# The last shared unit's second GEMM as three rounded products instead of native fp32, and the masks built in the first shared unit

## What is computed

```python
# layer 0: a softmax map from ctx, then a mixture of 8 experts and one shared expert
x = x + softmax(layernorm_affine(sim(layernorm(x), ctx)))
xt = layernorm(x)
top_p, top_i = top_k(softmax(xt @ gate_w), 2)      # each expert takes 160 slots per choice
h = gelu(buf[e] @ w1[e] + b1[e])                   # 256 -> 1024
y = h @ w2[e] + b2[e] + gelu(buf[e] @ wd[e]) @ wu[e]
sh = gelu(xt @ sw1 + sb1) @ sw2 + sb2 + gelu(xt @ swd) @ swu
x = x + sum_k(top_p[k] * y[expert k]) + 0.2 * sh
# layer 1: attention scores from ctx times layernorm(x), masked, softmax
scores = (ctx @ Wq.T + bq) @ (ctx @ Wk.T + bk).T / 8 * layernorm(x)
x = x + softmax(where(mask_SxS2 | mask_BxS2, -inf, scores))
# then a gated FFN whose weights are looked up in a table of 16
x = x + (silu(xn @ gate.T) * (xn @ up.T)) @ down.T
```

## Time and profile before

| | |
|---|---|
| median of three runs | 328.35 us |
| the profiled execution | 328.0 us, its span 326.3 us |
| TensorE busy (matmul) | 305.4 us, 94% of the span |
| VectorE, ScalarE, GpSimd busy | 239.2, 151.3, 111.6 us |
| mean granted TensorE clock | 0.965 |
| chain that ended last, by engine | PE 78%, DVE 9%, POOL 4%, ACT 3% |

### The profile page before, as it was taken

The page is one execution under the profiler, slowest core; times in us unless marked ns, Lnnn a source line. Parts: engine busy times, 40 slices in busy tenths (PEclk is TensorE's granted clock), DMA queues, the critical chain, the costliest instruction groups (busy, mean ns, idle before and its releaser), DMA issues.

```text
span 326.3 us, 6015 instructions
## 1 busy us (share of the span) xinstructions
PE 305.4 (94%) x1944; PEld 262.5 (80%) x1944; DVE 239.2 (73%) x650; ACT 151.3 (46%) x358; POOL 111.6 (34%) x153
## 2 busy tenths in 40 slices
PE   8998567997999999999999999999999989979995
PEld 4654355776989899898989999899888879879994
DVE  3658987413499989898998989898986749866632
ACT  2466437533346455564546555565633532541210
POOL 7473644770000605032150604123062226234331
PEclk9998769999899999999999999999999999979998
DMA  7994018335167664939375574828033000010101
GB/s 230 371 265 105 7 42 268 123 113 148 48 178 249 142 220 97 308 63 294 94 212 167 129 252 72 294 52 229 3 40 131 1 0 2 0 35 0 34 1 64
DMA packets 26259, 41.48 MB, mean 127 GB/s; under 512 B 3898, under 2 KB 16955, under 8 KB 26236
## 3 DMA queue, kind: packets, MB, share of 16 engines
q1 hardware_dynamic: 22012, 36.46, 35.2%
q0 software_dynamic: 4224, 4.75, 8.2%
HBM read 31.37 MB, written 9.82 MB: 126 GB/s over the span
## 4 chain that ended last, share of the span: by engine, by line
PE 78%; DVE 9%; POOL 4%; issue 3%; ACT 3%; DMA 1%; SPq 0%; POOLq 0%
PE hb L715 25%; PE yb L734 24%; PE hb L849 10%; PE yb L748 5%; PE tb L648 3%; PE rb L864 3%; PE yb L553 2%; POOL xbuf_dram L498 2%; PE yb L864 1%; DVE x L1249 1%; DVE bst L1104 1%; DVE xn L1110 1%; DVE xT_lo L1262 1%; POOL rstd L461 1%; DMA xbuf_dram<-xn,put_i 1%
## 5 line engine op out<-in xcount | busy, mean ns | idle before, releaser
L734 PE MATMUL yb<-raw,h 128*128 128x256 f32 x384 | 96.7, 382 | 0.0
L1015 ACT ACTIVATE h<-hb,b 128x320 f32<-128x320 f32 (+1 forms) x80 | 44.6, 559 | 70.1 <-PE hb L715 68.7
L734 PEld LDWEIGHTS yb<-raw,h 128*128 128x128 f32 x384 | 70.3, 192 | 7.5 <-ACT h L1015 0.4
L715 PE MATMUL hb<-xT_hi,w_hi 128*128 128x320 f32 (+1 forms) x180 | 72.6, 403 | 1.4 <-DVE xT_lo L1262 1.4
L518 POOL DMA_INDIRECT xacc_dram<-ysb,slot_i x16 | 25.5, 1594 | 126.1 <-ACT ysb L883 123.6
L715 PE MATMUL hb<-xT_lo,w_hi 128*128 128x320 f32 (+1 forms) x180 | 59.3, 329 | 0.0
L715 PE MATMUL hb<-xT_hi,w_lo 128*128 128x320 f32 (+1 forms) x180 | 59.2, 329 | 0.0
L1454 DVE TENSOR_TENSOR w_lo<-raw,w_hi 128x256 fp32r<-128x256 f32 x81 | 33.6, 415 | 22.3 <-ACT w_hi L883 22.2
L1136 DVE COPY_PREDICATED pick<-bits,pick 128x536 int32<-128x536 uint8 x56 | 42.7, 762 | 0.6
L715 PEld LDWEIGHTS hb<-xT_hi,w_hi 128*128 128x128 f32 x180 | 34.4, 191 | 6.6 <-issue 2.0
L715 PEld LDWEIGHTS hb<-xT_hi,w_lo 128*128 128x128 f32 x180 | 34.6, 192 | 2.5
(11 more groups left out here) (205 smaller groups left out, 523.4 us busy)
## 6 DMA issues: line engine op xcount, KB each, us to landing
raw<-w1pack_dram SPq DMA_DIRECT2D x30, 384.0 KB, 3.5
raw<-w2pack_dram SPq DMA_DIRECT2D x30, 384.0 KB, 5.5
xbuf_dram<-h SPq DMA_DIRECT2D x8, 323.8 KB, 10.0
idx<-idx_dram SPq DMA_DIRECT2D x8, 268.0 KB, 6.1
xg<-xbuf_dram SPq DMA_DIRECT2D x8, 259.0 KB, 5.9
x<-x_dram SPq DMA_DIRECT2D x4, 256.0 KB, 4.4
xacc_dram<-x SPq DMA_DIRECT2D x2, 512.0 KB, 7.0
x<-xacc_dram SPq DMA_DIRECT2D x4, 256.0 KB, 4.6
```

What stands on the lines that cost most here:

```text
L715: mm = pe.matmul(hb[s % RING][:, 0:n], w[:, s, k * P:(k + 1) * P], a[:, turn, k, 0:n], start=(i == 0), stop=(i == len(terms) - 1))
L734: mm = pe.matmul(yb[c // 2][:, (c % 2) * D:(c % 2 + 1) * D], h, w, start=(s == 0 and c % 2 == 0), stop=(s == STEPS - 1), skip_group_check= ...
L1015: act.activation(hidden(s - 1, shared, turn), bank[:, 0:n], ACT.Gelu, bias=b1[:, expert, s - 1:s])\
```

## The change

In unit 9, steps 1 to 8, `second` does three fp32r products for each block of 128 tokens instead of one fp32 matmul. For this, a new `last_split` on ScalarE rounds the step's w2 rows (128x256) and the hidden block (128x512), and a `last_split` on VectorE makes the low halves of both. The w2 halves lie in the rings `h_hi` and `h_lo`; the hidden halves lie in three slots, two in the half of `xT_hi` and `xT_lo` that unit 8 used, and one in the first two blocks of `w_hi` and `w_lo`. The masks are built at steps 5 to 8 of unit 0 and no longer at steps 0 to 4 of unit 9.

```diff
@@ PE second
-                if s > 0:
+                split = s > 0 and u_is(u, E + 1)
+                if split:
+                    pe.wait_ge(w2_lo_ok, s)
+                    pe.wait_ge(last_lo_ok, s)
+                elif s > 0:
                     pe.wait_ge(h32_ok, u * NF + s)
...
+                    if split:
+                        pairs = ((last_hi(s)[:, rows], last_w2_hi(s)), (last_hi(s)[:, rows], last_w2_lo(s)),
+                                 (last_lo(s)[:, rows], last_w2_hi(s)))
@@ ACT gelu
-                if shared:
+                if u_is(u, E + 1):
+                    if s > RING:
+                        act.wait_ge(last_lo_ok, s - RING)
...
@@ ACT
+            def last_split(s, g, turn):
+
+                act.wait_ge(raw2_in[turn][s // 3], (E + 1 - turn) * 8 + 16)
+                if s > RING:
+                    act.wait_ge(mm2, g - RING + 1)
+                copy(last_w2_hi(s), raw2[:, turn, s, :]).then_inc(w2_hi_ok, 1)
+                act.wait_ge(h32_ok, (E + 1) * NF + s)
+                copy(last_hi(s), hidden(s - 1, True, turn)).then_inc(last_hi_ok, 1)
+
@@ ACT unit, after gelu of the step and ahead of the next split_hi and of exps
+                    if s > 0 and u_is(u, E + 1):
+                        last_split(s, g, turn)
@@ DVE unit, ahead of combined and attend of the step
+                    if s > 0 and u_is(u, E + 1):
+                        last_split(s, u * STEPS + s, turn)
                     if s in (5, 6) and u_is(u, E + 1):
                         combined(s - 5)
                         attend(s - 5)
@@ DVE
+            def last_split(s, g, turn):
+
+                dve.wait_ge(w2_hi_ok, s)
+                if s > RING:
+                    dve.wait_ge(mm2, g - RING + 1)
+                dve.tensor_tensor(last_w2_lo(s), raw2[:, turn, s, :], last_w2_hi(s).bitcast(F32), ALU.subtract)\
+                    .then_inc(w2_lo_ok, 1)
+                dve.wait_ge(last_hi_ok, s)
+                dve.tensor_tensor(last_lo(s), hidden(s - 1, True, turn), last_hi(s).bitcast(F32), ALU.subtract)\
+                    .then_inc(last_lo_ok, 1)
+
@@ DVE unit0_extra
+                if s >= 5:
+                    build_mask(s - 5)
+                if s == 8:
+                    dead_rows()
@@ DVE tail
-                if s < B:
-                    build_mask(s)
-                if s == B:
-                    dead_rows()
                 if s == 7:
                     add_probs(1, 0, 4)
```

More of the change, by code:

```diff
@@ L256, in program @@
         mm2 = sem("mm2")
+        w2_hi_ok = sem("w2_hi_ok")
+        w2_lo_ok = sem("w2_lo_ok")
+        last_hi_ok = sem("last_hi_ok")
+        last_lo_ok = sem("last_lo_ok")
         third_mm = sem("third_mm")
@@ L290, in hidden, with last_w2_hi, last_w2_lo, last_part @@
             return h32[:, at:at + SLOTS]
+        def last_w2_hi(s):
+            return h_hi[:, s % RING, :]
+        def last_w2_lo(s):
+            return h_lo[:, s % RING, :]
+        def last_part(x_rows, weights, s):
+            at = (s - 1) % RING
+            return x_rows[:, 0, at, :] if at < 2 else weights[:, 0:2, :].rearrange("p a n -> p (a n)")
+        def last_hi(s):
+            return last_part(xT_hi, w_hi, s)
+        def last_lo(s):
+            return last_part(xT_lo, w_lo, s)
         def product(r):
@@ L729, in second @@
                     rows = slice(c * P, (c + 1) * P)
-                    if s > 0:
-                        h, w = hidden(s - 1, shared, turn)[:, rows], raw2[:, turn, s, :]
-                    else:
-                        h, w = lowrank[:, rows], w_up[:, :]
-                    mm = pe.matmul(yb[c // 2][:, (c % 2) * D:(c % 2 + 1) * D], h, w,
-                                   start=(s == 0 and c % 2 == 0), stop=(s == STEPS - 1), skip_group_check=True)
+                    if split:
+                        pairs = ((last_hi(s)[:, rows], last_w2_hi(s)), (last_hi(s)[:, rows], last_w2_lo(s)),
+                                 (last_lo(s)[:, rows], last_w2_hi(s)))
+                    elif s > 0:
+                        pairs = ((hidden(s - 1, shared, turn)[:, rows], raw2[:, turn, s, :]),)
+                    else:
+                        pairs = ((lowrank[:, rows], w_up[:, :]),)
+                    for i, (h, w) in enumerate(pairs):
+                        mm = pe.matmul(yb[c // 2][:, (c % 2) * D:(c % 2 + 1) * D], h, w,
+                                       start=(s == 0 and c % 2 == 0), stop=(s == STEPS - 1 and i == len(pairs) - 1),
+                                       skip_group_check=True)
                 mm.then_inc(mm2, 1)
@@ L1000, in gelu @@
                 act.wait_ge(mm1, g + 1)
-                if shared:
+                if u_is(u, E + 1):
+                    if s > RING:
+                        act.wait_ge(last_lo_ok, s - RING)
+                    elif s == 0:
+                        act.wait_ge(mm2, g - RING + 1)
+                    else:
+                        act.wait_ge(third_mm, E - 1)
+                elif shared:
                     if g >= RING:
```

## The result

The changed kernel takes 332.99 us (median of 20 runs, 330.73 to 337.53); the kernel before took 327.52 in the 20 runs beside it (325.55 to 332.02). The medians differ by 5.5 us. The ratio is 1.0174, 95% interval 1.0151 to 1.0197, taken without the few executions that ran in a slower state: slower by 5.7 us, clear of no change, but short of the 2% from which it counts as a difference here. The profiled execution of the changed kernel took 330.73 us, its span is 329.0.

A forecast was written before the change was run, and what follows sets the result against it. TensorE was taken as the bound, with a second chain through VectorE and ScalarE in unit 9 having hardly any room. Masks +0.6, chain +5.3 and clock +1.0 made +6.9 on 328.0, 335.3 us by the median; range 332.7 to 337.6.

The forecast's parts named there:

- TensorE's own work: Unit 9's second takes 1.42 us a step instead of 1.73, saving 0.31 a step, 2.5 us over eight.
- The splits while there is slack: In unit 9, second(1) to second(5) do not wait for copies and low halves; second(6) nearly as free.
- The chain from step 5 on: Unit 9's VectorE and ScalarE lists delay second(7) and second(8); transposes start 5.3 us later, TensorE's saving already counted.
- Masks: In unit 0 the fourth mask and dead rows delay unit 1's token halves, +0.6 us; unit 9 gains nothing.
- The clock: After idling in unit 9 TensorE runs at lower clock in second(8) or the first gate_ups, +1.0 us.
- wait but no clock loss: Rival: unit 9's wait comes without loss from a lower clock; +5.9 us, 334.2 us, chance 33%.
- the softened order: Rival: an unseen wait frees VectorE earlier, so add_probs is not in the way in unit 9; -2.4, 332.9 us, 5%.

The follow-up runs named there:

- split6_reorder: Kernel before with three products only in steps 1 to 6, masks at unit 0's steps 4 to 7, batch 1's softmax later; ratio 0.9933 to before.
- exps_late: Changed kernel with both batches' exponentials after gelu(8) and its copies, and add_probs(1, 0) behind step 8's low halves; ratio 1.0046 to before.
- attend_first: Changed kernel with VectorE's combined and attend ahead of the low halves at steps 5 and 6; ratio 1.0103 to before.
- split6: Changed kernel with three products only in steps 1 to 6 and masks at steps 4 to 7 of unit 0, softmax order kept; ratio 1.0104 to before.
- masks_only: Kernel before with masks and dead rows built at steps 5 to 8 of unit 0 and nothing split; ratio 0.9996 to before.
- changed_again: The changed kernel itself, word for word, run again as a yardstick; ratio 1.0182 to before.
- halves8_first: Changed kernel with VectorE's add_probs(1, 0) behind the low halves of step 8 instead of ahead of them; ratio 1.0241 to before.

## Why the prediction was right or wrong

The prediction was 335.3 us, 2.1% slower; measured were 332.99 and 1.74%. Its mechanism stood in every step; its +6.9 us was a fifth to a quarter too large against the measured 5.5 to 5.7. It gave 0.57 to a loss of over 2% and 0.39 to one within 2%, and the less likely of the two came. The measured time lies only 0.3 us above the lower end of its range, 332.7.

- **TensorE's own work:** right. second(s) takes 1.42 us (split6_reorder saves 1.86 us with six steps, 6 x 0.31). By an estimate from the four passes that the Trainium skill ("FP8 and Floating Point Precision", "TensorE Precision Notes") gives for fp32, six steps would save 6 x 0.43 = 2.6; the trace shows 1.86.
- **The splits while there is slack:** right, no wait ahead of second(1) to second(6).
- **The chain from step 5 on:** right, in place and size. Forecast was a wait of 5.9 us ahead of second(7), of 0.5 to 2 ahead of second(8), and the transposes 5.3 us later; measured are 5.70, 0.35 and 5.37. The second wait is shorter than forecast because second(7) took 2.9 us at half clock and not 2.5. VectorE was idle for 3.65 us behind `nmx` of batch 1, not for over 4. exps_late, attend_first and split6 each change one link and move the wait as the chain says. The 5.37 contain second(8)'s slower clock, 0.3, so the chain alone is 5.1. With 0.39 for the masks the two terms make 5.8, where the ratio gives 5.7 and the medians 5.5. That they meet so closely is in part luck: a single profile stands against the medians, and the half-clock stretches elsewhere are worth 1.5 us each.
- **Masks:** mis-sized. +0.6 was forecast, 0.39 is what the profile shows, and where the rows come late from DRAM it is 0 (masks_only: 0.9996). Of the 0.57, 0.2 was not there because VectorE ended w_up at 78.56 and not at 78.77. And I took the time at which unit 1's rows land as fixed to VectorE's, while it differs from one execution to another: the transposes started at 78.69 in the profile of the change and at 80.80 in changed_again.
- **The clock:** mis-sized. +1.0 was put on top. The clock did fall to half after the wait, but second(7) had room for it, second(8) lost 0.3 (0.1 in changed_again), and the first `gate_up`s ran at full speed. The loss that was forecast for these is real elsewhere: in exps_late, attend_first and halves8_first part of them ran at half clock. At unit 1 and around 290 to 300 us the half-clock stretches came and went between two executions of the changed kernel; of the kernel before there is one profile, which has both.
- **Rivals:** by its mechanism "wait but no clock loss" (334.2) comes nearest, with masks at 0.4 and not at 0.6. By the number alone the nearest is the softened order (332.9), and that is a coincidence: `add_probs` did stand in the way, from 260.63 to 262.95 in VectorE's list.

The profiled execution of before was 0.35 us below the first median and is 0.5 above that of 20 runs, so 0.8 us of the difference between 335.3 and 332.99 is in the base.

## What to carry to other kernels

Before work is taken off the busiest engine, follow the next chain through the same stretch: here gelu(7) was ready just when TensorE wanted it, so a faster TensorE could gain nothing, and the helper instructions from step 5 on, put into the in-order lists of the other engines, made the chain longer. Those of steps 1 to 4 fell into idle time and cost nothing. Ask for each added instruction what stands behind it in its engine's list, and above all for loops between engines, as here VectorE, ScalarE, VectorE, ScalarE, VectorE. Then move the long independent work behind the urgent, and apply the cheaper form only to the steps that have slack: six steps of eight gained 0.7%, eight gained nothing, and eight in the old order lost 1.7%.

## What the runs showed of the hardware

A full-clock stretch is not a property of the kernel: the changed program had the half-clock stretch at unit 1 in changed_again and not in its first profile, and units 1 to 8 took 156.01 and 154.47 us. Half clock behind a wait can cost nothing: second(7) took 2.9 instead of 1.65 us while the next operands were still 3.25 us away. ScalarE's table load for the exponentials ran ahead of the wait for their input (at 249.67 in the changed kernel, 0.31 us of wait left at 251.26), so only the load on the way back to gelu, 1.28 us, lay on the chain. After the same kind of wait in unit 9 the clock was back at full when the first `gate_up`s ran (the change, changed_again) or dropped to half again in them (halves8_first, 0.50 from 274 to 276 us).
